# Graph layer pair: two of a turn's 36 row gathers replaced by ScalarE column copies and a TensorE projection

## What is computed

```python
h = jnp.maximum(_layernorm(x, axis=-1), 0.0)
...
filters = jax.nn.silu(edge_attr @ fW1 + fb1) @ fW2 + fb2      # 206250 x 128
messages = (x[src] @ dW + db) * filters                        # x is h here
aggregated = jax.ops.segment_sum(messages, dst, num_segments=x.shape[0])
upd = jax.nn.silu(aggregated @ uW1 + ub1) @ uW2 + ub2
return x + upd
```

## Time and profile before

| | |
|---|---|
| median of 2 runs | 4104.41 us (4102.91 to 4105.91) |
| span of the profiled execution | 4098.5 us, 63699 instructions |
| PE busy | 3358.1 us (82%) |
| POOL busy | 3050.9 us (74%) |
| DVE busy | 2405.1 us (59%) |
| ACT busy | 1368.9 us (33%) |
| indirect gathers, convolution | 1592, 1509.2 us busy, 491.6 us idle ahead of them |

### The profile page before, as it was taken

How to read it: one execution, slowest core, us unless ns; L and a number is a source line. 1 busy time by engine, 2 the same in 40 slices (tenths; PEclk the granted TensorE clock), 3 DMA queues, 4 the chain that set the end, 5 groups by cost and what they waited for, 6 DMA issues and landing times. The chain is left out here.

```text
span 4098.5 us, 63699 instructions
## 1 busy us (share of the span) xinstructions
PE 3358.1 (82%) x14005; PEld 2625.3 (64%) x14006; DVE 2405.1 (59%) x5327; ACT 1368.9 (33%) x3398; POOL 3050.9 (74%) x3216
## 2 busy tenths in 40 slices
PE   5788888888888888888768898888888888888798
PEld 3566666666666666666656676766766666666676
DVE  7888888888888888888853333333333332333333
ACT  5455555555555555555421111111111111111111
POOL 6777777777777777777757777777777777777776
PEclk7555555555555555555567666667666677667767
DMA  4222222222222222222232222222222222222222
GB/s 125 58 60 61 61 60 61 62 60 61 61 60 61 61 61 60 61 61 59 59 88 78 79 74 78 79 74 78 75 77 78 75 78 78 74 79 74 78 78 62
DMA packets 190049, 288.10 MB, mean 70 GB/s; under 512 B 85904, under 2 KB 132811, under 8 KB 185384
## 3 DMA queue, kind: packets, MB, share of 16 engines
q0 software_dynamic: 101888, 212.13, 20.6%
q1 hardware_dynamic: 83160, 33.99, 3.5%
q10 hardware_dynamic: 4840, 40.55, 3.2%
HBM read 271.07 MB, written 12.49 MB: 69 GB/s over the span
## 5 line engine op out<-in xcount | busy, mean ns | idle before, releaser
L63 POOL DMA_INDIRECT ce_xg<-table,ce_idx x1592 | 1509.2, 948 | 491.6 <-issue 481.5
L63 POOL DMA_INDIRECT ae_xg<-table,ae_idx x1592 | 1502.5, 944 | 491.2 <-issue 489.6
L1496 DVE TENSOR_TENSOR ce_msg<-ce_ring,ce_xg 128x768 f32<-128x768 f32 x269 | 257.6, 958 | 1151.0 <-DMA ce_xg<-table,ce_idx 1150.6
L948 PE MATMUL ae_ps_k<-ae_xg,ae_e 128*96 128x129 f32 x3224 | 882.7, 432 | 0.0
L1417 PEld LDWEIGHTS ce_ring<-ce_fw,ce_hid 128*128 128x128 f32 x3228 | 586.6, 278 | 435.6 <-DVE ce_msg L1496 314.6
L1417 PE MATMUL ce_ring<-ce_fw,ce_hid 128*128 128x128 f32 x3228 | 649.6, 377 | 262.1 <-DVE ce_msg L1496 261.8
L948 PEld LDWEIGHTS ae_ps_k<-ae_xg,ae_e 128*96 128x96 f32 x3224 | 689.6, 277 | 126.7 <-issue 117.2
L1387 ACT ACTIVATE ce_hid<-ce_ps_h,ce_fb 128x768 f32<-128x768 f32 x269 | 241.8, 899 | 1235.4 <-PE ce_ps_h L1441 692.2
L1441 PE MATMUL ce_ps_h<-ce_ea,ce_fw 50*128 50x384 f32 x1076 | 548.3, 641 | 19.0 <-DMA ce_ea<-in_edge_attr 17.1
L1426 PEld LDWEIGHTS ce_ring<-ce_hot,ce_msg 128*128 128x128 f32 x3224 | 528.4, 253 | 3.0 <-DVE ce_msg L1496 2.9
L1426 PE MATMUL ce_ring<-ce_hot,ce_msg 128*128 128x32 f32 x3224 | 514.3, 319 | 1.0 <-DVE sums L1504 1.0
(11 more groups left out here) (186 smaller groups left out, 3336.2 us busy)
## 6 DMA issues: line engine op xcount, KB each, us to landing
ae_stage<-table SPq DMA_DIRECT2D x2560, 0.5 KB
ce_stage<-table SPq DMA_DIRECT2D x2560, 0.5 KB
ce_ea<-in_edge_attr ACTq DMA_DIRECT2D x88, 450.0 KB
ae_xg<-table,ae_idx POOLq DMA_INDIRECT x1592, 2.5
ce_xg<-table,ce_idx POOLq DMA_INDIRECT x1592
sums<-in_x SPq DMA_DIRECT2D x7, 448.0 KB, 4.6
table<-sums SPq DMA_DIRECT2D x6, 462.0 KB, 3.5
pj_bias<-in_x_rows SPq DMA_DIRECT2D x42, 64.0 KB
```

The source lines that it names most:

```text
L63: eng.indirect_dma_start(out=out, out_offset=None, in_=table[:, :], in_offset=bass.IndirectOffsetOnAxis(ap=idx, axis=0)).then_inc(done, 16)
L948: last = nc.tensor.matmul(ps_k[0:KEYS, 0:D + 1], by_chunk[s % 3][:, c, :], xg[:, s % XS, c, 0:D + 1], start=(c == 0), stop=(c == count - 1))
L1496: nc.vector.tensor_tensor(msg[:, s % 3, :, :], filt, xg[:, s % XS, :, :], ALU.mult).then_inc(s_msg, 1)
```

## The change

In turns 2 to 44 of the convolution, the last chunk of slots 1 and 3 is no longer gathered by POOL (`TO = [1, 3]`). Instead the turned, normalised features of all nodes are kept on chip (`by_node`, 128 partitions x 6272 nodes), and ACT copies one column of 128x1 for each of the chunk's 128 edges into `held`. PE multiplies `held` by `dW`. DVE adds `db` and writes the result into the chunk's place in `xg`. ACT does this one turn ahead, in turns 1 to 43: 48, 48 and 32 columns in three units for the one chunk, and the same in the other three units for the other. The node numbers lie on chip as 16-bit integers; ACT loads eight of them at a time into registers, and the first of the eight is always at a multiple of 16 bytes.

For that the attention stores each turned tile as well (`features`, one more DMA on SP per turn), the convolution loads `features` back in its first turn (one DMA of 3.2 MB), and `prepare` makes the 16-bit list (one POOL copy of 86x128, two DMAs). The diff, cut to its core:

```diff
+COLUMNS = (Column((0, 1, 2), 5, 1), Column((3, 4, 5), 2, 3))
+COLUMN_TURNS = TURNS - 2
+TO = [column.to for column in COLUMNS]
+BATCHES = ((0, 48), (48, 96), (96, 128))
+FETCH = 8
...
+def sources_at(nc, engine, columns, i, m, first):
+    return nc.values_load_multi_w_load_instructions(columns[:, bass.ds(((i - 1) * len(COLUMNS) + m) * P + first, FETCH)], engines=[engine],
+                                                    min_val=0, max_val=N - 1, skip_runtime_bounds_check_because="a source is a node")[1]
...
 def gather_units(...)
-                taken = carried is not None and s == CARRY_SLOT
+                taken = carried is not None and s == CARRY_SLOT or s in to and not (isinstance(i, int) and i < 2)
...
 def attention_edges(...), SP
-                    sp.dma_start(messages[bass.ds((i - OPEN - 1) * P, P), :], p.turned).then_inc(stored, 16)
+                    sp.dma_start(messages[bass.ds((i - OPEN - 1) * P, P), :], p.message).then_inc(stored, 16)
+                    sp.dma_start(features[:, bass.ds((i - OPEN - 1) * P, P)], p.turned).then_inc(stored, 16)
...
 def convolution_edges(...), SP
+            def tables(r):
+                sp.wait_ge(scaled, 1)
+                sp.wait_ge(project.last_turned, 16)
+                sp.wait_ge(s_column, r * COLUMN_TURNS * len(COLUMNS) + len(COLUMNS))
+                sp.dma_start(by_node, features[:, :]).then_inc(table_in, 16)
...
 ACT, behind the Silu of each unit
+                        if collects(i):
+                            collect(i, s)
+                def collect(i, s):
+                    m = s // 3
+                    e0, e1 = BATCHES[s % 3]
+                    if s % 3 == 0:
+                        act.wait_ge(s_column, column_at(r, i, m) + 1)
+                        act.sem_inc(begun, 1)
+                    if s == 0:
+                        act.wait_ge(table_in, 16 * (r + 2))
+                        act.sem_inc(begun, 1)
+                    for e in range(e0, e1, FETCH):
+                        nodes = sources_at(nc, mybir.EngineType.Activation, columns, i, m, e)
+                        for k, node in enumerate(nodes, e):
+                            last = nc.scalar.copy(held[:, m, k:k + 1], by_node[:, bass.ds(node, 1)])
+                    if s % 3 == 2:
+                        last.then_inc(s_other, 1)
...
 PE
+                def products(i, m, b):
+                    k = column_at(r, i, m)
+                    pe.wait_ge(s_other, k + 1)
+                    nc.tensor.matmul(ps_x[b], held[:, m, :], project.dw[:, :], start=True, stop=True).then_inc(s_column, 1)
...
 DVE
+                def place(i, m, b):
+                    column = COLUMNS[m]
+                    dve.wait_ge(s_column, column_at(r, i, m) + 1 + len(COLUMNS))
+                    dve.wait_ge(s_msg, r * UNITS + i * SL + column.to + 1 + XS)
+                    nc.vector.tensor_tensor(xg[:, column.to, CH - 1, :], ps_x[b], project.db, ALU.add).then_inc(s_placed, 1)
```

More of the change, by code:

```diff
@@ L537, in __init__, with collects, places, column_chunks @@
         self.chunks = (span * SL * np.arange(1, carried + 1) + CARRY_SLOT) * CH + CH - 1
+class Column:
+    def __init__(self, collected, placed, to):
+        self.collected, self.placed, self.to = collected, placed, to
+        self.late = placed < collected[-1]
+COLUMNS = (Column((0, 1, 2), 5, 1), Column((3, 4, 5), 2, 3))
[3 more added lines that the diff above has]
+FETCH = 8
+STORES = 48
+def collects(i):
+    return not (isinstance(i, int) and not 1 <= i <= COLUMN_TURNS)
+def places(i, column):
+    first = 2 if column.late else 1
+    return not (isinstance(i, int) and not first <= i < first + COLUMN_TURNS)
+def column_chunks():
+    turn = np.arange(2, TURNS)
+    return np.stack([(turn * SL + to) * CH + CH - 1 for to in TO], 1).reshape(-1)
+def column_at(r, i, m):
+    return r * COLUMN_TURNS * len(COLUMNS) + (i - 1) * len(COLUMNS) + m
 LOAD = 3
@@ L1268, in __init__ @@
         self.w, self.dw, self.bias = sb("w", [P, NT, D]), sb("dw", [P, D]), sb("bias", [P, NT, D])
-        parts = sb("parts", [P, 3, D])
-        self.relu, self.turned, self.db = (parts[:, k, :] for k in range(3))
+        parts = sb("parts", [P, 4, D])
+        self.relu, self.turned, self.db, self.message = (parts[:, k, :] for k in range(4))
         self.rows, self.x = (self.bias[:, k, :] for k in (1, 2))
@@ L1324, in convolution_edges @@
         carry = Carry(sb, lambda name: sem("c_" + name), CONVOLUTION, D, project, lists, table)
-        (w_in, pool_turn, steps, key_ready, begun, cleared, s_hid, s_act, s_flt, s_bias, s_msg, s_sum, s_acc) = (
-            sem("c_" + k) for k in "w_in pool_turn steps key_ready begun cleared hid act flt bias msg sum acc".split())
+        (w_in, steps, key_ready, begun, cleared, s_hid, s_act, s_flt, s_bias, s_msg, s_sum, s_acc) = (
+            sem("c_" + k) for k in "w_in steps key_ready begun cleared hid act flt bias msg sum acc".split())
+        columns = sb("columns", [1, COLUMN_TURNS * len(COLUMNS) * P], u16)
+        held = sb("held", [P, len(COLUMNS), P])
+        ps_x = [ps_f[b][:, 1024 - P:1024] for b in range(2)]
+        table_in, s_other, s_column, s_placed = (sem("x_" + k) for k in "table_in other column placed".split())
         merged, out_done, y_in, s_u, s_up_hid, s_v, s_up_bias, s_y = (sem("f_" + k) for k in "merged out_done y_in u hid v bias y".split())
@@ L1415, in filters @@
                         nc.tensor.matmul(tile_y, one_hid[:, :], update.w2[:, :], start=True, stop=True).then_inc(t_v, 1)
+                    for m, column in enumerate(COLUMNS):
+                        if at is not None and at[1] == column.placed and places(at[0], column):
+                            products(at[0] - 1 if column.late else at[0], m, b)
                     for c in range(CH):
@@ L1443, in turn @@
                         if not (first and s < 1):
-                            filters(n - 1, (s - 1) % SL, first and s < 3, i if s else None)
+                            filters(n - 1, (s - 1) % SL, first and s < 3, i if s else None, (i, s))
                         if not (first and s < 3):
@@ L1485, in one_hot, with aside, messages @@
                                             keys.unsqueeze(2).to_broadcast([P, CH, W]), ALU.is_equal)
-                def messages(n, s, i, carried, j=0):
+                def place(i, m, b):
[3 more added lines that the diff above has]
+                    nc.vector.tensor_tensor(xg[:, column.to, CH - 1, :], ps_x[b], project.db, ALU.add).then_inc(s_placed, 1)
+                def aside(r, at):
+                    if at is None:
+                        return
+                    i, s = at
+                    for m, column in enumerate(COLUMNS):
+                        if s == column.placed and places(i, column):
+                            place(i - 1 if column.late else i, m, (s - 1) % SL % 2)
+                def messages(n, s, i, carried, j=0, at=None):
                     filt = ps_f[s % 2][:, 0:CH * D].rearrange("p (c f) -> p c f", c=CH)
@@ L1492, in messages @@
                         update_tile(i)
+                    aside(r, at)
                     dve.wait_ge(s_bias, n)
                     carry.landed(dve, r, s, carried)
-                    dve.wait_ge(gathered[s], landed_by(carry.pace, r, i, s, carried, j))
+                    for m, to in enumerate(TO):
+                        if s == to and not (isinstance(i, int) and i < 2):
+                            dve.wait_ge(s_placed, column_at(r, i - 1, m) + 2)
+                    dve.wait_ge(gathered[s], landed_by(carry.pace, r, i, s, carried, j, TO))
                     nc.vector.tensor_tensor(msg[:, s % 3, :, :], filt, xg[:, s % XS, :, :], ALU.mult).then_inc(s_msg, 1)
```

70 lines of the change are left out of this document (44 added, 26 removed).

## The result

The changed kernel took 6192.65 us (2 runs, 6192.23 to 6193.08) against 4104.41 us before: a ratio of 1.5085, interval 1.5057 to 1.5114. I had forecast 4414 us with a range to 4820. The direction and the bound were right, the size was not: ACT's turn is 93.2 us long, where I had 51.0. The time is close to the rival that I had given one chance in five, "the eight values come one by one", 6422 us.

The account below looks back on a forecast made before the run. POOL bounds before, at 44.4 us a turn; ACT's instruction queue was to bound after, at 51.0. 4104 + 284 (43 turns) + 23 (column table) + 3 (list and last store) = 4414 us, range 3995 to 4820.

Parts of the forecast that it names:

- The direction and the bound: The kernel gets slower, 4414 us from 4104, with ACT's instruction queue bounding the convolution in place of POOL.
- the eight values come one by one: Rival: a register load on ACT takes 1.84 us, a turn 97.7, the kernel 6422; chance 0.20, outside the range.
- the one sentence on the register load: ACT's load of eight aligned 16-bit values counts as one 16-byte block, 0.38 us, 32 times a turn.
- The rest of the sum: ACT's turn: 32 x (0.10 + 0.38 + 8 x 0.12) = 46.1, plus 2.8 + 1.5 + 0.6: 51.0 us.
- The loop's end: ACT's loop body grows to 603 instructions; its jump is charged 2.8 us a turn, taken from SP's loop.
- the Silus with their register instructions: Six Silus a turn on ACT's queue, 0.1 us each, 0.6 us in all.
- The pairs: Address instruction plus 128x1 copy on ACT's queue: 0.12 us each, 256 a turn, 30.7 us.
- The rival in the engine: ACT's copies don't overlap: 203 ns each, 57.8 us a turn, kernel 4706 us; part of a shared chance of 0.60.
- ACT's own DMA issues: Two DMA issues a turn block ACT's queue for 0.74 us each, 1.5 us.
- The table: The 3.2 MB column table, issued in turn 0, arrives about 2159 us; ACT, asking at 2136, stands 23 us, once.
- Products and additions: PE's 86 products of about 0.4 us and DVE's 86 additions of 0.29 are hidden; without cover 34 + 25 us.
- Slower by over 2%: The whole kernel slows by more than a 2% step (82 us): 0.80, against same 0.10 and faster 0.10.

Follow-up runs that it names:

- the run without loads: The changed kernel without ACT's register loads and address instructions, copying 128 fixed columns for each chunk: 3998.2 us.
- the kernel with 315 instructions: The changed kernel with one chunk a turn in place of two, in units 1 to 5, 16-bit list, eight values per load: 4439.8 us.
- the shared kernel: The changed kernel with a 32-bit list, sixteen words per load, and DVE copying 48 of each chunk's 128 columns: 3993.4 us, ratio 0.9733.

## Why the prediction was wrong

**The step that failed** is the one sentence on the register load: "Eight 16-bit values at a multiple of 16 are just such 16 bytes. I take 0.38." The load takes 1.716 us. I had read from the earlier trace rows that the start of the block decides, and took the block to be counted in bytes. All rows there are of 4-byte words, so they could not tell bytes from words, and I said so only under the rival. The runs show that values of 2 bytes have no quick path. The other half of the rule, the start, was right: words moved by one take 1.751.

**The rest of the sum held, in part by luck.** With 1.72 in place of 0.38 the sum gives 32 x (0.10 + 1.72 + 0.96) + 4.9 = 93.9 us a turn; measured 93.2. But two of its errors cancel. A load with its address instruction and eight pairs takes (4007.9 - 4002.7) / 2 = 2.6 us, not 2.78. Line 506 of the kernel after, 4002 to 4010 us:

```profile
L506 ACTq TENSOR_LOAD <-ce_columns x3: 1716/1718/1731, 4002.7 to 4007.9; - x3
```

 At 2.62 us, the figure that stands in the expectations, 32 of them are 83.8 us, which leaves 9.4 us of the turn for what I had put at 4.9. The loop's end and the DMA issues below are 5.1 of these; some 4 us are left for the Silus with their register instructions and for the pauses among the pairs that are told at the end, where I had 0.6. The terms:

- *The pairs:* 0.10 us rather than 0.12. Eight address instructions of the kernel after, on line 1472:

```profile
L1472 ACTq FUSED_REGOPS  x8: 46/46/51, 4004.4 to 4005.1; - x8
L1472 ACT COPY ce_held<-sums x8: 191/191/192, 4004.5 to 4005.2; 128x1 f32 x8
```

 Seven steps in 0.7 us. The copies are 191 ns long and 0.10 apart, so they overlap, as the earlier trace rows let expect. The rival in the engine falls with it. The 0.10 is the pace of the queue: without address instructions 48 copies take 4.53 us, (4.53 - 0.19) / 47 = 0.092 each. The timeline of ACT in that kernel (the run without loads):

```profile
3004.76 4.53 ACT L1471 COPY ce_held<-sums 128x1 f32<-128x1 f32 x48
```

 The Trainium skill, ScalarE: Activation LUTs, section "What ACT_TABLE_LOAD costs", gives 186 ns + 0.833 ns per element for an ACTIVATE without pointer operands and 93 ns of overlap, an estimated 187 and 94 ns. The trace agrees for these copies: 191 ns in the kernel after, 92 apart in the run without loads.

- *The loop's end:* 2.5 us, where I took 2.8 from SP. The kernel after, line 530, 3999.4 to 4002.5 us:

```profile
L530 ACTq COMPARE_BRANCH  x1: 54/54/54, 3999.5 to 3999.5; - x1
L530 ACTq FUSED_REGOPS  x1: 119/119/119, 4002.0 to 4002.0; - x1
```

 In the kernel with 315 instructions it was 0.2. In the shared kernel, whose ACT body has some 367, it is 5.6:

```profile
L530 ACTq COMPARE_BRANCH  x1: 54/54/54, 3052.5 to 3052.5; - x1
L530 ACTq FUSED_REGOPS  x1: 119/119/119, 3058.1 to 3058.1; - x1
```

 So the price begins between 315 and some 367 instructions, and it doesn't grow with the length alone. That POOL bounds in the shared kernel hides it there. From 2300 to 3900 us the DMA queue of instructions moved 148 packets in the kernel after (17.2 turns) and 52 in the one with 315 instructions (30.6 turns). Its rows, as packets, MB and share of the DMA engines:

```profile
q14 instruction: 148, 1.21, 0.2%
...
q14 instruction: 52, 0.43, 0.1%
```

 The Trainium skill, Runtime: NRT & Kernel Launch, section "Instruction fetch mechanics", says that a taken branch to a target outside the two blocks that an engine keeps must fetch it first. The packets agree with that, 8.6 a turn against 1.7; why the price is highest at 367 instructions stays open.

- *ACT's own DMA issues:* 1.30 us rather than 0.74 (see the end). *The table:* ACT's first copy followed its last Silu by 14 us (from 2134 to 2148), of which 1.7 are the load, so the wait was some 12 us where I had 23.

- *Products and additions:* 0.8 us (two matmul records of 0.50 that overlap), where I had 0.4, and 0.28; hidden, as the run without loads shows.

**The chances.** Slower by over 2%: 0.80, and it was. But the case that came had 0.20 and lay outside the range. What spoke for it was in my own rows: the quick path had been seen for 4-byte words alone. The time per register that I had quoted from the Trainium skill, Runtime: NRT & Kernel Launch, section "Instruction fetch mechanics", about 200 ns, is the one that came out here: 208 ns for a 16-bit value. I let rows of another data type overrule it.

## What to carry over

Before an engine is given many small operations with addresses from memory, price the register loads by data type and start address, from a row of the same type; where there is none, the estimate has two ends and the slow one deserves as much weight. Keep such lists as 4-byte words at multiples of 16 bytes: eight values took 0.55 us so, and 1.72 as 16-bit values. Then count what is left: with the cheapest loads, ACT alone was still too slow, and the work had to be shared. Read an engine's own queue, not its busy share: ACT was busy for 42% of the span and bounded the convolution.

## What the runs showed of the hardware

- On ACT a register load takes 0.208 us for each 16-bit value, and about 0.24 us for each four 32-bit words that begin at a multiple of 16 bytes. On DVE the words are as quick (sixteen: 1.100 us, 1.024 on ACT); 16-bit values were loaded on ACT alone.
- ACT's DMA issue became longer: a median of 1.299 us in the kernel after, where it was 0.738 before. The row of the kernel after:

```profile
L1437 ACTq DMA_DIRECT2D ce_ea<-in_edge_attr x88: 740/1299/1417, 2116.1 to 6134.7; - x88
```

 Copies in flight are not the cause. In the run without loads an issue took 0.74 us while copies ran, and with one chunk a turn and 32-bit words one took 1.21 us although the engine had been idle since 2899.65 us. The timelines of ACT, first of the one and then of the other:

```profile
2898.84 2.14 ACT L1471 COPY ce_held<-sums 128x1 f32<-128x1 f32 x22
2900.87 0.74 ACTq L1437 DMA_DIRECT2D ce_ea<-in_edge_attr  x1
...
2905.59 1.21 ACTq L1438 DMA_DIRECT2D ce_ea<-in_edge_attr  x1
2906.91 0.90 ACT L1455 ACTIVATE ce_hid<-ce_ps_h,ce_fb 128x768 f32<-128x768 f32 x1 [7.26 <-issue]
```

 The issue is longer in the kernels whose ACT loads registers and makes addresses for its copies; which of the two does it stays open.
- Some groups of eight pairs take 0.3 us more than the others. In the kernel after, the eight from 4009.7 us need 1.0 us where those from 4004.4 need 0.7:

```profile
L1472 ACTq FUSED_REGOPS  x8: 46/46/46, 4009.7 to 4010.7; - x8
```

 These pauses stand at the same places of every turn: counted in ACT's recorded instructions from the loop's branch, behind number 48, 304, 432 and 560. The distances are multiples of 128, so the place in the program decides and not the data. What ACT waits for there stays open.
